# Sliding-window attention block on one core: float32 scores from the whole contraction, 256 columns a product, loop written out

## The reference

```
x = x + attention(layernorm(x)) ;  x = x + ffn(layernorm(x))

q, k, v = xWq+bq, xWk+bk, xWv+bv          # 16 heads of 8 features
scores  = q k^T / sqrt(8)                 # allowed: j <= i and i - j < 32
out     = softmax(masked scores) v        # then  out Wo + bo

m1, m2  = outer products of tokens 1..16  # a low-rank update of W1 and W2
h       = gelu(x W1^T + scale x m1^T + b1)    # 512 hidden
y       = h W2^T + scale h m2^T + b2
```

## Time and profile before

| | |
|---|---|
| median of 3 runs | 150.88 us (150.65 to 152.91) |
| the profiled execution | 152.15 us |
| its span, first to last instruction | 150.4 us |
| busy in the span: PE, DVE, ACT, POOL | 121.7, 108.7, 89.7, 51.5 us |
| mean granted TensorE clock | 0.941 of full |

### The profile page before, as it was taken

How to read it: one execution, slowest core, us unless ns; L and a number is a source line. 1 busy time by engine, 2 the same in 40 slices (tenths; PEclk the granted TensorE clock), 3 DMA queues, 4 the chain that set the end, 5 groups by cost and what they waited for, 6 DMA issues and landing times.

```text
span 150.4 us, 4925 instructions
## 1 busy us (share of the span) xinstructions
PE 121.7 (81%) x1859; PEld 100.9 (67%) x1859; DVE 108.7 (72%) x281; ACT 89.7 (60%) x256; POOL 51.5 (34%) x78
## 2 busy tenths in 40 slices
PE   0757089689978959987887996898799999999992
PEld 0316058579967848877777895787667557676892
DVE  6588867947899698699879879999998734111021
ACT  3427318879488675758769758837944774242400
POOL 7287828980060051015006003140830089500000
PEclk9999999555999996899998799999999999999999
DMA  1693896894716749716665952980000000010122
GB/s 45 191 287 132 277 249 236 203 352 147 191 67 238 190 129 335 205 44 240 197 163 192 255 145 89 306 197 10 0 4 0 7 0 0 23 51 26 43 67 73
DMA packets 27311, 21.08 MB, mean 140 GB/s; under 512 B 1303, under 2 KB 23070, under 8 KB 27294
## 3 DMA queue, kind: packets, MB, share of 16 engines
q1 hardware_dynamic: 27294, 20.85, 45.9%
HBM read 10.88 MB, written 9.96 MB: 139 GB/s over the span
## 4 chain that ended last, share of the span: by engine, by line
PE 42%; DVE 23%; ACT 10%; issue 10%; DMA 8%; SPq 3%; POOL 2%; DVEq 1%; ACTq 0%; POOLq 0%
PE bank_o L476 7%; PE bank_s L454 6%; DVE probsT L827 6%; PE bank_qk L595 5%; PE bank_s L499 5%; ACT V L612 4%; DVE negmax L810 4%; DMA KS<-k_scr 4%; PE bank_v L595 4%; PE bank_o L499 3%; DVE centred L818 3%; PE bank_qk L418 2%; DVE k_parts L804 2%; DMA q_scr<-q_parts 2%; DVE rest L791 2%
## 5 line engine op out<-in xcount | busy, mean ns | idle before, releaser
L454 PEld LDWEIGHTS bank_s<-KS,QS 128*128 128x128 bf16 x512 | 35.9, 164 | 3.4 <-DVE centred L818 2.3
L454 PE MATMUL bank_s<-KS,QS 128*128 128x64 bf16 x512 | 35.8, 228 | 2.0 <-DVE centred L818 1.7
L476 PE MATMUL bank_o<-V,probsT 128*32 128x36 f32 x1024 | 25.0, 207 | 9.6 <-DVE probsT L827 9.6
L476 PEld LDWEIGHTS bank_o<-V,probsT 128*32 128x32 f32 x1024 | 21.5, 119 | 14.9 <-issue 9.0
L810 DVE TENSOR_REDUCE negmax<-bank_s 128x8 f32<-128x512 f32 x32 | 21.9, 683 | 10.6 <-PE bank_s L454 10.5
L612 ACT ACTIVATE V<-bank_v 32x64 f32<-32x64 f32 x128 | 27.5, 215 | 1.5
L668 ACT ACTIVATE probs<-centred 128x512 f32<-128x512 f32 x32 | 20.0, 629 | 6.0 <-DVE probsT L827 5.2
L827 DVE STREAM_TRANSPOSE probsT<-probs 128x512 f32<-128x512 f32 x32 | 22.5, 702 | 0.1
L281 POOL TENSOR_TENSOR q_parts<-rest,q_parts 128x256 bf16<-128x256 f32 x8 | 6.0, 748 | 48.2 <-ACT q_parts L612 48.2
L818 DVE TENSOR_TENSOR centred<-bank_s,negmax 128x512 f32<-128x512 f32 x32 | 21.3, 665 | 0.2
L612 ACT ACTIVATE attT<-bank_w,bias_cols 128x128 f32<-128x128 f32 x16 | 5.9, 369 | 9.9 <-PE bank_w L518 9.9
(11 more groups left out here) (105 smaller groups left out, 219.7 us busy)
## 6 DMA issues: line engine op xcount, KB each, us to landing
k_scr<-k_parts SPq DMA_DIRECT2D x8, 576.0 KB, 4.3
KS<-k_scr SPq DMA_DIRECT2D x8, 576.0 KB, 5.9
q_scr<-q_parts SPq DMA_DIRECT2D x8, 512.0 KB, 3.3
QS<-q_scr SPq DMA_DIRECT2D x32, 128.0 KB, 2.9
x_sb<-in_L_attn_x_dram SPq DMA_DIRECT2D x1, 768.0 KB, 5.4
out_dram<-y SPq DMA_DIRECT2D x3, 256.0 KB, 2.3
w<-in_L_ffn_W_dram SPq DMA_DIRECT2D x2, 256.0 KB, 5.4
x_sb<-in_L_attn_x_dram SPq DMA_DIRECT2D x2, 128.0 KB, 2.3
```

The lines of the kernel that those rows point to most:

```text
L454: mm = nc.tensor.matmul(dst, QS[b][:, o, g].rearrange("p h t -> p (h t)")[:, j::BLOCKS], KS[b][:, o, g, j * WIN:(j + 2) * WIN], start=(o = ...
L476: mm = nc.tensor.matmul(o[q * WIN:(q + 1) * WIN, g * VC:(g + 1) * VC], probsT[s % 2][:, i, g, w, :], V[b][:, j + w, g, :], start=(w == 0), ...
```

## The change

The bfloat16 parts, the scratch tensors and their DMAs are gone. Scores are float32 products over all 128 rows. For one block, `Qm` holds the transposed Q four times, once for each head of a group, each time with only the rows of those heads (`copy_q`, ACT, 4 copies of 128x256 a chunk, scale = `head_of`, a column of ones and zeros). `Kx` holds K once per group with the other groups' rows at zero, over the whole sequence. One product then gives the scores of a block for all 4 groups: 128 stationary columns and 256 moving ones, 2 a unit. The mask comes first, as one bfloat16 product of 512 columns of an identity with `band`.

K goes through `k_sb` (ACT `copy_k`) and 4 small DMAs a chunk that put each group's 32 rows into `Kx` (chunk 0: 4 DVE copies). POOL zeroes `Kx` beforehand, and now clears all of `V` (three rings of 8 blocks) before it writes its ones.

There are 4 score banks and rings of 4 for `negmax`, `centred`, `probs` and `probsT`. `values` handles 4 blocks at once (32 products), the block changing fastest. `project_v` writes V spread over heads: 32 products of 32 stationary and 32 moving columns, so that `spread_v` is 4 copies of 32x256. `denominators`, `normalise`, `turn_att`, `copy_attT`, `out_proj` and `residual` handle 2 tiles at a time. All loops are written out. The feed-forward part is the same work; its `values` lag is two units.

```diff
-                    for g in range(NG):
-                        dst = bank_s[s % 2][:, (i * NG + g) * 2 * WIN:(i * NG + g + 1) * 2 * WIN]
-                        for o in range(2):
-                            mm = nc.tensor.matmul(dst, QS[b][:, o, g].rearrange("p h t -> p (h t)")[:, j::BLOCKS],
-                                                  KS[b][:, o, g, j * WIN:(j + 2) * WIN],
-                                                  start=(o == 0), stop=(o == 1),
...
+                ge(pe, centred_done, k - 3)
...
+                    nc.tensor.matmul(bank_s[k % 4][:].rearrange("p (n k) -> p n k", k=KW), ident_bf[:],
+                                     band[:, 0:1].to_broadcast([P, UB * NG, KW]),
+                                     start=True, stop=False, skip_group_check=True)
+                for i in range(UB):
+                    j = UB * u + i
+                    k0 = c * CHUNK + j * WIN
+                    mm = nc.tensor.matmul(out_s[:, i], Qm[c % 2][:, j].rearrange("p h q -> p (h q)"),
+                                          Kx[:, :, k0:k0 + KW], start=False, stop=True, skip_group_check=True)
...
+                for g in range(NG):
+                    for w in range(2):
+                        for q in range(QB):
+                            key = (BLOCKS * c + QB * t + q - 1 + w) % (RING * BLOCKS)
+                            mm = nc.tensor.matmul(bank_o[c % 2][q * WIN:(q + 1) * WIN,
...
+                for j in range(BLOCKS):
+                    for hh in range(GH):
+                        mm = nc.tensor.matmul(bank_b[hh * WIN:(hh + 1) * WIN, CHUNK + j * WIN:CHUNK + (j + 1) * WIN],
+                                              xT[c % 2][:, j * WIN:(j + 1) * WIN], cols[:, hh],
...
+            def turn_x(c):
+                pe.wait_ge(xn_done, c + 1)
+                ge(pe, v_done, GH * c)
...
+            for c in range(1, NCH):
+                sp.wait_ge(k_done, c + 1)
+                sp.wait_ge(k_zero, c + 1)
+                for g in range(NG):
+                    rows = slice(g * WIN, (g + 1) * WIN)
+                    sp.dma_start(Kx[rows, g, WIN + c * CHUNK:WIN + (c + 1) * CHUNK],
+                                 k_sb[c % 2][rows]).then_inc(k_in[c % 2], 16)
...
             ln1_rstd(1, 0, TILES)
+            nc.gpsimd.memset(Kx[:, :, 0:WIN + CHUNK], 0.0).then_inc(k_zero, 1)
             ln1_rstd(2, TILES, 2 * TILES)
+            for r in (0, 2, 1):
+                nc.gpsimd.memset(V[:, r * BLOCKS:(r + 1) * BLOCKS], 0.0).then_inc(zeroed, 1)
+                if r == 2:
+                    nc.gpsimd.memset(Kx[:, :, WIN + CHUNK:WIN + 2 * CHUNK], 0.0).then_inc(k_zero, 1)
+                    ln1_rstd(3, 2 * TILES, 4 * TILES)
+            pool.wait_ge(zeroed, RING)
+            for hh in range(GH):
+                nc.gpsimd.memset(V[hh * WIN:(hh + 1) * WIN, :, :, GH * HD + hh:GH * HD + hh + 1],
+                                 1.0).then_inc(v_one, 1)
```

More of the change, by code:

```diff
@@ L30 @@
 GH = 4
+UB = 2
 NG = HEADS // GH
@@ L106, in block_kernel @@
         xT = two("xT", [P, CHUNK])
[L107 to L121, removed]
+        Qm = two("Qm", [P, BLOCKS, GH, WIN])
+        k_sb = two("k_sb", [P, CHUNK])
+        Kx = sb("Kx", [P, NG, WIN + S])
+        V = sb("V", [P, RING * BLOCKS, NG, VC])
+        R = 4
+        negmax, centred, probs = ([sb(f"{n}{i}", [P, width]) for i in range(R)] for n, width in (
+            ("negmax", UB * NG), ("centred", UB * NG * KW), ("probs", UB * NG * KW)))
+        probsT = [sb(f"probsT{i}", [P, UB, NG, 2, WIN]) for i in range(R)]
+        rden = sb("rden", [P, TILES, NG, GH])
+        att = sb("att", [P, TILES, D])
+        attT = sb("attT", [P, CHUNK])
         stats2 = sb("stats2", [P, NT, 6])
@@ L579, in _ @@
-            scores(0, 0)
-            turns(pe, body)
-            for s in range(SU, SU + 6):
-                step(SUPER - 1, s, True)
             def down(f):
                 pe.wait_ge(hidden_done, HC * (f + 1))
+                if f < 2:
+                    pe.wait_ge(x1_done, NCH - 1 + f)
                 ge(pe, y_done, f - 1)
@@ L700, in step @@
[L700 to L716 removed]
+            copy_q(0, range(GH))
@@ new lines, in _ @@
+            for k in range(NS + 7):
+                c, g = k // UNITS, k % UNITS
+                if k < NS:
+                    row_max(k)
+                if k < NS:
+                    centre(k)
+                if 1 <= k < NS + 1:
+                    turn_probs(k - 1)
+                if g == 2 and 1 <= c <= NCH:
+                    denominators(c - 1)
+                    normalise(c - 1)
+                if g == 1 and 2 <= c:
+                    residual(c - 2)
+                if g == 2 and 2 <= c:
+                    ln2_stats(c - 2)
+                if k == 0:
+                    dve.wait_ge(rstd1_done, 3)
+                    ln1_norm(2)
+                    ln1_var(4 * TILES, NT)
+                if g == 2 and c in (3, 5, 7):
+                    ln2_var((c - 3) // 2)
+                if k == NS - 5:
@@ L943, in step @@
                     copy_x2T(0)
-                if last and s == 6:
+                if k == NS - 2:
                     update_weights()
-                if last and s == 9:
+                if k == NS + 1:
                     copy_x2T(1)
-                    ln2_var(2)
-                if s < SU and p1 and u == 2:
-                    repeat_high(2 * turn + b + 2, b)
-            def body(turn):
-                for s in range(SU):
-                    step(turn, s, is_last(turn))
-            turns(dve, body)
@@ L957, in _ @@
-            for s in range(SU, SU + 7):
-                step(SUPER - 1, s, True)
             ln2_var(3)
```

810 lines of the change are left out of this document (310 added, 500 removed).

## The result

| | before | changed |
|---|---|---|
| median, measured side by side | 150.76 us (149.81 to 152.91, 4 runs) | 142.62 us (141.47 to 144.98, 4 runs) |
| ratio | | 0.945 (0.933 to 0.958) |
| profiled execution, its span | 152.15, 150.4 us | 141.82, 140.1 us |
| mean granted clock | 0.941 | 0.951 |
| busy PE, DVE, ACT, POOL | 121.7, 108.7, 89.7, 51.5 | 109.7, 93.6, 70.8, 45.7 us |

A forecast was written before the change was run, and what follows sets the result against it. Bound: a ring of waits between PE and DVE, then PE's tail. Unit 4 at 29.7, seven chunks 70.7 and one-off work 2 give 102.4; the tail ends at 136.6, plus 2 for waits: span 138.6, predicted 139 us, range 132.5 to 147.5.

The forecast's parts named there:

- A, the forecast: Whole kernel: the summed estimate holds, 134 to 143 us; chance 0.48.
- Unit's scores, 1.07: PE, each unit: two float32 products of 0.43 us plus a mask product of 0.21, against 0.95 before.
- Rival E: PE scores: float32 loads are not hidden, adding 1.8 us a chunk; chunk 11.3, total 147 to 148 us; chance 0.04.
- 32 products of `values`, 1.1: PE, each tile: small products take 1.1 us, between bounds of 0.65 (four quarters at once) and 1.3.
- rival C: Whole kernel: everything overlaps, four quarters at once, DVE dense at 9.2 us, unit 4 at 28.5; 131 to 132; chance 0.15.
- PE 9.5 a chunk: Middle: PE's work per chunk at full clock sums to 9.5 us, with bounds 8.4 to 10.1.
- Rival B: Middle: PE or K's way to the scores sets the pace, chunk 11.2 us, total 146 to 147; chance 0.22.
- K's ring 9.2, landing 2.3: Middle: K's copy, DMA issues, landing of 2.3 us and PE work up to the next projection close a 9.2 us loop.
- Chunk 10.1: Middle: three nearly equal loops (DVE, PE, K) do not mesh exactly, so a chunk takes 10.1 us against 12.0.
- Start, unit 4 at 29.7: Start: DMA round trips go, a wait for POOL's ones comes in; unit 4 at 29.7 us, 4.6 earlier.
- Tail: End: DVE leaves unit 31 at 102.4 us; PE's remaining work of 32.9 from 100.4, then 0.5 and 2.8, ends at 136.6.
- rival D: Whole kernel: slower, because float32 products suffer from TensorE's lower clock level; 154 us or more; chance 0.11.

The follow-up runs named there:

- V-wait run: Changed kernel with ACT's V copies waiting only for the first tile's `values` of the chunk two back instead of both tiles; 141.44 us, ratio 0.935.
- version of three edits: Changed kernel with V copies released earlier, the first third of V's ones first, and the `attT` copy ahead of the last exponential; 133.97 us, ratio 0.893.
- `attT` run: Changed kernel with ACT's copy of chunk 6's transposed attention output moved ahead of the last exponential; 137.64 us, ratio 0.911.
- the ones first: Changed kernel with POOL clearing the first third of V and writing its ones before the rest of V; 136.82 us, ratio 0.904.
- The additions: Changed kernel plus 35 unread DVE additions of 128x256, five in each of 7 chunks; 156.86 us, ratio 1.030.

## Why the prediction was right, and where it was not

Predicted 139 us, range 132.5 to 147.5; measured 142.62. The rival that came out is A, the forecast, at the slow side of its 134 to 143. Of the 3.6 us between forecast and median 1.5 lie in the span (138.6 forecast, 140.1 measured). The rest is the spread of executions: the forecast took its 11.8 off the median before, but the profiled execution before lay 1.3 above its median, the profiled one of the changed kernel 0.8 below. Step by step:

- **Unit's scores, 1.07.** Measured 1.08, no load in sight. Rival E is out. They are dearer than the 0.95 of before, as the sum said.
- **32 products of `values`, 1.1.** Wrong in size: 0.70, the lower bound and so rival C's term; V's 32 too (0.69 to 0.77). I had taken the end "nearer to the row there is", a row in which two quarters take turns. The run with one quarter after the other shows it. The lower bound of the chunk was also added up wrongly: with 0.65, 0.65 and 0.6 the terms give 8.1, not 8.4.
- **PE 9.5 a chunk.** The pieces of the chain, with the fourth unit's scores, sum to 8.7; busy are 9.1 (42.46 over 4.66 chunks). Rival B is out with this.
- **DVE 9.1 to 9.5.** 44.44 over 4.66 chunks is 9.5.
- **K's ring 9.2, landing 2.3.** 32 KB land in 1.9, but three issues take 1.87 (0.6 each) instead of 0.45 each. The ring does wait (6.3 us in all), which by the prediction's own list was a sign of a wrong step; trading it for ACT copies changes nothing, and once V's wait is loosened it is the one wait left in the chain of the middle.
- **Chunk 10.1.** Measured 10.3. PE's term was 0.4 to 0.8 too high, which changed nothing, since DVE's 9.5 stands beside it. "Do not mesh exactly" was put at 0.6 above the largest term and was 0.8. The four banks, named there as a help, had no part in it before the last two chunks.
- **Start, unit 4 at 29.7.** Measured 29.93. First V copy forecast at 16.8, found at 17.35, released by POOL, as the start's fence shows. The last 0.8 comes by another way than summed: unit 4's scores are done at 29.2, and DVE reaches them at 29.93. What I didn't see is that this wait was the dearest thing left in the kernel: 5.8 us.
- **Tail.** The failed step. Unit 31's transposition was to leave DVE at 102.4; the transpositions of units 30 and 31 end at 103.7. From there the sum gives 34.2 (136.6 - 102.4), measured are 36.4 (140.1 - 103.7). The run with the copy moved has 32.5 from the same event (103.2 to 135.7), so the sum of PE's work was 1.7 too high, and the wait, 3.9 with the clock that goes with it, was left out. I had costed the copy at 0.5, by its duration, and not asked what stands ahead of it on ACT: an exponential that waits for DVE's last centring. The 2 us "for waits that I can't place" and the 1.7 too much hid this between them; that is luck, not foresight.
- **The clock, rival D.** In the middle it was 1.00 where it had been 0.93, so D is out, but the lower level came twice after the first products: from 14.2 to 24.4 us and from 103.0 to 106.4, so that 96 to 108 us has 0.86, another of the prediction's signs of a wrong step. PE had been idle for 1.1 us at the first fall and for 3.7 at the second; in the kernel before it fell at 26.9, though PE had been busy 2.35 of the 2.9 us from 24.0 on.

The gain, then: DVE's work fell from 10.45 to 9.5 us a chunk (41.80 in four chunks; 44.44 in 4.66), its idle time from 1.6 to 0.8, together the 1.7 of the chunk. The first part is the splitting that went. By the timeline of the kernel before its five instructions hold DVE 1.8 us a chunk:

```profile
65.66 0.48 DVE L791 SCALAR_TENSOR_TENSOR rest<-bank_qk,bias_cols,q_parts 128x256 f32<-128x256 f32 x1
66.05 0.48 DVE L794 SCALAR_TENSOR_TENSOR rest<-bank_qk,bias_cols,k_parts 128x256 f32<-128x256 f32 x1
...
67.07 0.26 DVE L799 COPY q_parts<-q_parts 128x512 bf16<-128x512 bf16 x1
67.24 0.28 DVE L800 COPY k_parts<-k_parts 128x512 bf16<-128x512 bf16 x1
67.44 0.70 DVE L804 COPY k_parts<-k_parts 128x256 bf16<-128x256 bf16 x1
```

Only 0.9 of it shows, since from 48 to 96 us DVE now also does work of the second layer norm (`mv`, `var`, `x2T`, 0.4 us a chunk) that the kernel before had outside that stretch, and the three instructions of a unit pack a little less densely (1.87 us against 1.80, 0.3 a chunk). The second part goes with PE's cheaper small products: with them undone DVE idles again. That this is all of it is argued, not shown.

Open: what holds the chunk once V's wait is loosened. From unit 12 to 24 it takes 9.7 us in the V-wait run and in the version of three edits (46.0 to 75.2), where DVE is busy 28.26 of 29.2 us; there the chain goes through PE and waits for K of 1.06 to 1.36. So it is DVE, or PE with K's ring; no run took work from DVE or K's wait away without loading ACT.

## What to carry to other kernels

For each copy that an edit leaves in place or puts in at the start and the end, read what stands ahead of it in its engine's queue and when that is released, not only how long the copy lasts: two such places, each a matter of order alone, were worth more than any ring in the middle. Let small products change the column quarter each time; the same products in another order cost 2.7 times as much. When two engines are both near 90% busy, taking a wait away moves it to the next one, while 70 to 85% of the work added to either shows.

## What the runs showed of the hardware

- 32 float32 products with 32 stationary and 36 moving columns take 0.70 us over four column quarters and 1.91 over one after the other.
- Float32 loads of 128 columns hide completely behind products of 256 columns: a unit's four records take 0.86, half of the 1.72 for four records of twice the columns, and the mean load lasts 195 ns beside them.
- Every run starts at the lower level of TensorE's clock (0.50, 1.2 GHz), though the clock column says 1.00: it counts the time before the first recorded change as full. The four records of a unit's scores tell the level. In the changed kernel they take 1.91 us at 19.95, where the column has 0.50. In the `attT` run, whose column has 1.00 from 14 to 24 us:

```profile
19.87 1.91 PE L352 MATMUL bank_s<-Kx,Qm 128*128 128x256 f32 x4
23.98 1.03 PE L352 MATMUL bank_s<-Kx,Qm 128*128 128x256 f32 x4
```

- With the same wait of PE for ACT's copies at the start, the clock rose to full at 24.4 us in the changed kernel's execution, at 22.8 in the V-wait run's and at 22.5 in the `attT` run's; unit 4 came at 29.9, 29.2 and 28.9, so 2 us at the lower level cost about 1 us. With the ones first, where PE is back at work at 13.9, it rose at 15.2. The Trainium skill, "TensorE: Matmul & The Clock Gate", section "What's actually happening", has the throttled state as the default, which activity releases. The starts agree with it; what these traces add is that executions in which PE has the same work differ in the moment by 2 us, and that the changed kernel's alone had full speed before that as well, from 10.8 to 14.2.
- The additions took 591 ns each in the mean where others of 128x256 take 415 in the changed kernel (`residual`). Of the 35, 25 take 0.38 to 0.42 us and 10 take 0.61 to 1.49. All 10 run beside work of POOL on `xn` or `x_bo`, and the three groups of 1.72 us beside an idle POOL. That POOL's work is the cause was not tried.
